# A decoder layer on one core: cross probabilities of two batches in one tile, 64-row output products, and steps that stand elsewhere

## The chip, the cores and the metric

The kernel runs on one core of a Trainium2 chip. The metric is the device time of one execution in microseconds (us), the median of several runs. Before the change it is 665.8 us, the median of three runs (664.77, 665.8 and 667.24). The profile shown below is one more execution, which took 664.33 us. Its span, from the first instruction to the last, is 662.6 us.

## The reference, cut to what matters

x has 16 batches of 256 rows with 128 features, the context 16 batches of 64 rows. The layer is a causal self-attention with 16 heads, a cross-attention with one head, and a feed-forward network of eight experts whose outputs are weighed by an entmax gate. Each part is added to x.

```python
x = x + attn(_layernorm(x))            # 16 heads of 8, causal, its own layernorm before Wo
# cross-attention: k = v = ctx, q = layernorm(x)
scores = einsum('bqd,bkd->bqk', qp, kp) * scale
probs  = softmax(scores, axis=-1)      # over the 64 context rows of the query's own batch
ctx    = einsum('bqk,bkd->bqd', probs, vp)
x = x + einsum('bqd,ed->bqe', ctx, Wo) + bo
...
gates = entmax_bisect(logits)          # exact threshold over 8 experts here
h = relu(einsum('td,edf->etf', xt, W1) + b1)
y = einsum('etf,efd->etd', h, W2) + b2
x = x + einsum('etd,te->td', y, gates)
```

## The kernel before

The batches are worked on in eight pairs (512 rows, as four tiles of 128). A pair passes through three parts: Z (layernorm, projections, row maxima of the scores), A (the rest of the self-attention, the cross-attention) and X (gates and experts). The parts are a software pipeline: a round does X of one pair, A of the next and Z of the one after that. A first phase without X fills the pipeline. Then come rounds 1 to 6 with all three parts (2 to 6 are a hardware loop), round 7 with X and A, and round 8 with X alone. YT adds a pair's expert output.

Each engine has its own program in order, made from the tables `Z_STEPS`, `A_STEPS` and `X_STEPS`. A row has a step, its number, its PSUM bank and, for each engine that takes part, a number: the whole part is a slot (0 to 33), and the fraction orders the steps within it. In slot t TensorE runs the first product of chunk t (called F(t) below: three 512-column matmuls into `h_ps`), the steps with a fraction under .5, the second product of chunk t-2 (S(t-2), three matmuls into `y_ps`), and then the steps with .5 or more. ScalarE rounds the hidden rows (H(t)), VectorE makes their remainder (L(t), `h_lo`). F(t) and S(t-2) wait for L(t-2). Nothing is reordered at run time: a step that waits holds up everything behind it on its engine.

The steps that the change touches:

- SC n: scores of two heads each (an even and an odd n together fill banks s and t); ScalarE takes exponentials into `prob`, GpSimd masks them (L902, each mask adds one to `prob_made`).
- TH 0 to 2: GpSimd's threshold for the gates (L934 to L964), after LG's logits on TensorE and VectorE.
- PV n: value products. Each has two halves; the second half of PV1 waits until the masks of SC6 and SC7 are made.
- MAX n: score maxima. An even and an odd n are one block of TensorE in banks s and t, four groups of 32 rows side by side; VectorE reduces each (L1657). A block waits until both banks were read by their last readers. MT: the maxima are transposed and split (L1664, L1666).
- XS, PT, XO: cross scores, the transposes of the exponentials `cp` and the product with `vo` (values times output matrix). `cp` has one 128x128 block for each of the four tiles, and a batch's 64 context rows fill only its half of it (`h0`): the other half is zero. PT transposes four blocks, ScalarE and VectorE split all 512 columns, and XO makes three products for each tile. VectorE adds XO's result to x1 (L1698).
- SA, NA, T3: statistics, normalisation and transposes; T3's split `fT_hi`, `fT_lo` feeds F(0) of the next round. SZ: statistics of the pair in Z.

PSUM has eight banks: s and t of two banks each, m, two of `h_ps`, one `y_ps`. A step takes a bank when all earlier users of it are drained.

```python
h0 = (k // 2) * C
last = act.activation(cp[:, k, h0:h0 + C], ps_of[buf][:, k * C:(k + 1) * C], ACT.Exp, ...)
```

Of the kernel before, what the change touches and what calls it, by code (L numbers as in the profile page):

```python
# [65 lines left out]
class Step(NamedTuple):  # L66
# [64 lines left out]
    Step("SA", 1, "-", dve=20.01, pool=4.75),
    Step("NA", 1, "-", act=23.01),
    Step("T2", 0, "m", pe=24.51, act=24.01, dve=24.01),
    Step("XS", 0, "m", pe=26.01, act=26.01, dve=25.01),
    Step("PT", 0, "s", pe=27.02, act=27.01, dve=26.04),
    Step("SA", 2, "-", dve=28.04, pool=6.25),
    Step("XO", 0, "m", pe=28.52, dve=28.03),
    Step("NA", 2, "-", act=31.01),
    Step("T3", 0, "m", pe=32.52, act=31.02, dve=31.02),
    Step("RL", 0, "-", sp=1),  # L140
]
# [3 lines left out]
    Step("LG", 0, "s", pe=1.01, dve=1.01),  # L145
    Step("TH", 1, "-", pool=1.25),
# [266 lines left out]
def bass_decoder_layer(nc, x, ctx_in, wq, wk, wv, wo, gamma, beta, xwk, xwv, xbv, xwq, xbq, xwo, xbo,  # L413
# [6 lines left out]
    with ctx:  # L420
# [15 lines left out]
        zeros = sb("zeros", [NJ, 1, P])  # L436
# [1376 lines left out]
```

## Time and profile before

| | us |
|---|---|
| median of three runs | 665.8 |
| profiled execution | 664.33 |
| its span | 662.6 |
| ahead of round 1's first F(0) | 100.16 |
| round 6 (467.24 to 540.80) | 73.56 |
| round 7 (540.80 to 607.43) | 66.63 |
| round 8 and the end (607.43 to 662.60) | 55.17 |

TensorE is busy 618.6 us, 93% of the span, VectorE 70%, ScalarE 62%, GpSimd 55%. The granted TensorE clock is 0.991 in the mean. Rounds 2 to 6 repeat within 0.15 us, so one of them, round 6, is read for all. A matmul's shown duration overlaps the next one's: what a matmul costs is read from start to start.

### The profile page before, as it was taken

How to read it: one execution, taken by the hardware profiler on the slowest of the kernel's cores; microseconds unless marked ns; L12 is line 12 of the kernel's file. 1: busy time of each engine (PE TensorE's matmuls, PEld its weight loads, DVE VectorE, ACT ScalarE, POOL GpSimd, SP SyncE). 2: the span in 40 equal slices, each digit the busy share in tenths (PEclk: the TensorE clock that was granted, in tenths of full speed). 3: DMA queues.
4: the chain of work that ended last, by engine and by line, in shares of the span. 5: the costliest groups of instructions: out<-in, count | busy, mean ns of one | idle time of the engine just before them, and what ended most of it. 6: DMA issues, size and time to landing. Idle time of an engine off the chain costs nothing.

```text
span 662.6 us, 15729 instructions
## 1 busy us (share of the span) xinstructions
PE 618.6 (93%) x5263; PEld 459.8 (69%) x5263; DVE 464.3 (70%) x996; ACT 408.0 (62%) x780; POOL 363.9 (55%) x599
## 2 busy tenths in 40 slices
PE   5488879999999999999999999999999999998997
PEld 3355557777677767777678767777677767776775
DVE  4495984679747986689747986599557984656544
ACT  4239476755777566755766557755776567665543
POOL 8625565445663737444763746544753756464363
PEclk9889999999999999999999999999999999999999
DMA  6705100530027000630036000720045000700230
GB/s 187 230 17 169 45 4 18 127 117 4 19 45 208 10 8 14 151 107 2 18 67 191 0 20 0 162 95 2 18 98 159 2 2 6 159 2 1 55 88 16
DMA packets 39195, 43.76 MB, mean 66 GB/s; under 512 B 2922, under 2 KB 23670, under 8 KB 39158
## 3 DMA queue, kind: packets, MB, share of 16 engines
q1 hardware_dynamic: 39158, 43.28, 24.5%
q8 instruction: 22, 0.36, 0.2%
q14 instruction: 15, 0.12, 0.1%
HBM read 10.04 MB, written 2.10 MB: 18 GB/s over the span
## 4 chain that ended last, share of the span: by engine, by line
PE 77%; DVE 8%; ACT 6%; POOL 3%; issue 2%; DMA 2%; SPq 2%; ACTq 0%; DVEq 0%; POOLq 0%
PE h_ps L1038 10%; PE y_ps L1038 9%; PE h_ps L1040 8%; PE h_ps L1039 8%; PE y_ps L1040 8%; PE y_ps L1039 8%; DVE negmax L1657 5%; PE sbuf_m L1149 5%; PE sbuf_s L1132 3%; PE sbuf_s L1104 2%; ACT prob L1462 2%; PE sbuf_s L1149 2%; PE sbuf_s L1053 1%; PE sbuf_s L1066 1%; PE sbuf_m L1038 1%
## 5 line engine op out<-in xcount | busy, mean ns | idle before, releaser
L1773 DVE SCALAR_TENSOR_TENSOR h_lo<-h_ps,h_hi 128x512 fp32r<-128x512 f32 x256 | 172.2, 682 | 120.3 <-ACT h_hi L1481 119.4
L1481 ACT ACTIVATE h_hi<-h_ps 128x512 fp32r<-128x512 f32 x256 | 152.1, 601 | 129.7 <-PE h_ps L1040 127.7
L1038 PE MATMUL h_ps<-fT_lo,w_hi 128*128 128x512 f32 x256 | 111.6, 436 | 4.1 <-DVE fT_lo L1626 2.7
L902 POOL TENSOR_SCALAR_AFFINE_SELECT prob<-prob 128x512 f32<-128x512 f32 x128 | 79.8, 642 | 60.7 <-ACT prob L1462 57.2
L1462 ACT ACTIVATE prob<-sbuf_s 128x768 f32<-128x768 f32 x124 | 95.2, 813 | 25.7 <-PE sbuf_s L1132 25.7
L1038 PE MATMUL y_ps<-h_lo,w_hi 128*128 128x512 f32 x255 | 106.9, 419 | 1.5 <-ACT y_sb L1490 1.5
L1657 DVE TENSOR_REDUCE negmax<-sbuf_s 128x4 f32<-128x1024 f32 (+1 forms) x91 | 106.9, 1212 | 0.1
L1039 PE MATMUL h_ps<-fT_hi,w_lo 128*128 128x512 f32 x256 | 101.2, 395 | 0.0
L1040 PE MATMUL h_ps<-fT_hi,w_hi 128*128 128x512 f32 x256 | 101.1, 395 | 0.0
L1040 PE MATMUL y_ps<-h_hi,w_hi 128*128 128x512 f32 x255 | 100.8, 395 | 0.0
L1039 PE MATMUL y_ps<-h_hi,w_lo 128*128 128x512 f32 x255 | 100.7, 395 | 0.0
L909 POOL TENSOR_TENSOR vareps_a<-mv_a,eps_t 128x4 f32<-128x4 f32 (+1 forms) x27 | 5.4, 200 | 157.5 <-DVE mv_a L1592 157.5
L983 POOL TENSOR_TENSOR y_sb<-y_sb,gate_b 128x512 f32<-128x512 f32 x55 | 70.9, 1290 | 11.9 <-ACT y_sb L1490 11.9
L986 POOL TENSOR_TENSOR acc<-acc,y_sb 128x512 f32<-128x512 f32 x55 | 70.7, 1286 | 4.3
L1038 PEld LDWEIGHTS h_ps<-fT_lo,w_hi 128*128 128x128 f32 x256 | 48.0, 188 | 19.9 <-DVE fT_lo L1626 4.0
L1038 PEld LDWEIGHTS y_ps<-h_lo,w_hi 128*128 128x128 f32 x255 | 47.9, 188 | 17.8 <-DVE h_lo L1773 3.5
L1040 PEld LDWEIGHTS h_ps<-fT_hi,w_hi 128*128 128x128 f32 x256 | 48.1, 188 | 11.5
L1040 PEld LDWEIGHTS y_ps<-h_hi,w_hi 128*128 128x128 f32 x255 | 47.9, 188 | 11.5
L1039 PEld LDWEIGHTS y_ps<-h_hi,w_lo 128*128 128x128 f32 x255 | 48.1, 188 | 7.6
L1490 ACT ACTIVATE y_sb<-y_ps,biasT 128x512 f32<-128x512 f32 x63 | 43.6, 691 | 15.5 <-PE y_ps L1040 13.1
L1039 PEld LDWEIGHTS h_ps<-fT_hi,w_lo 128*128 128x128 f32 x256 | 48.3, 189 | 6.3
L1149 PE MATMUL sbuf_m<-prob,v_t 128*32 128x128 f32 (+1 forms) x704 | 33.2, 329 | 0.0
(449 smaller groups left out, 1046.2 us busy)
## 6 DMA issues: line engine op xcount, KB each, us to landing
gate_b<-gT SPq DMA_DIRECT2D x64, 256.0 KB, 4.9
stacks<-qk SPq DMA_DIRECT2D x42, 256.0 KB, 2.5
gate_b<-in_L_ffn_W_dram SPq DMA_DIRECT2D x8, 512.0 KB, 6.1
x_r<-in_x_dram SPq DMA_DIRECT2D x8, 256.0 KB, 4.0
x_t<-in_x_dram SPq DMA_DIRECT2D x7, 256.0 KB, 2.7
out_dram<-sums SPq DMA_DIRECT2D x7, 256.0 KB, 4.4
w_hi<-qk SPq DMA_DIRECT2D x3, 256.0 KB, 4.5
w_lo<-qk SPq DMA_DIRECT2D x3, 256.0 KB, 5.4
```

The source lines that it names most:

```text
L902: pool.affine_select(out=v, in_=v, compare_op=ALU.is_ge, fill=0.0, base=0, pattern=[[0, 2], [0, 2], [1, P]], channel_multiplier=-1).then_i ...
L983: mark(pool.tensor_tensor(y, y, gate_b[:, e, :], ALU.mult))
L986: pool.tensor_tensor(acc[:, :], acc[:, :], y, ALU.add).then_inc(summed, 1)
L1038: pe.matmul(out_ap, w_hi, m_lo, start=start, stop=False)
L1039: pe.matmul(out_ap, w_lo, m_hi, start=False, stop=False)
L1040: return pe.matmul(out_ap, w_hi, m_hi, start=False, stop=stop)
L1149: last = pe.matmul(o[:, 0:S] if first else o[:, P:S], tile[:, c:c + VW], blocks(prob[:, (2 * n + v) % PG, j, :], first), start=first and v ...
L1462: act.activation(pair_of_heads(n), halves[buf][:, :, 0:3 * P], ACT.Exp).then_inc(free[buf], 1)
L1481: act.activation(h_hi[:, c % HB, :], h_ps[:, c % 2, :], ACT.Relu).then_inc(hhi_made, 1)
L1490: act.activation(y_sb[:, e % YB, :], y_ps[:, :], ACT.Identity, bias=biasT[:, e:e + 1]).then_inc(y_made, 1)
L1657: dve.tensor_reduce(negmax[:, tile, :].rearrange("p (j g) -> p j g", g=NG)[:, j:j + 2, gs], halves[buf].rearrange("p j (g s) -> p j g s", ...
L1773: dve.scalar_tensor_tensor(out=h_lo[:, c % HB, :], in0=h_ps[:, c % 2, :], scalar=0.0, in1=h_hi[:, c % HB, :], op0=ALU.max, op1=ALU.subtrac ...
```

## The change

- `cp`: in the rounds the tiles k and k+2, one of each batch, share a block (`k % 2`), since their context rows fill different halves. PT then makes two transposes in place of four, and its split has 256 columns in place of 512.
- XO: each of the two batches has its 64 rows of the array. Twelve products of 64 rows and 128 columns replace twelve of 128 rows; the two batches go to the two banks of s, where one bank (m) held all before.
- VL, a new step on SyncE's queue behind RL and ahead of K, copies the pair's rows of `vo_hi` and `vo_lo` to a fixed tile `vo_now` (two transfers from SBUF to SBUF); XO waits for it.
- The memset of `zeros` goes; the transfer that clears rows of the stacks reads a row of the stacks. `odd` and `tilt` lie in another tile.
- Many steps get other numbers. T1, PT and TA move to bank m, Q to t, XO to s, BT 2 and 3 change places.

```diff
-    Step("PT", 0, "s", pe=27.02, act=27.01, dve=26.04),
+    Step("PT", 0, "m", pe=27.02, act=26.0118, dve=27.0385),
...
-    Step("XO", 0, "m", pe=28.52, dve=28.03),
+    Step("XO", 0, "s", pe=28.52, dve=28.5248),
...
+    Step("VL", 0, "-", sp=1.1),
...
-            if s.name not in SPLIT_HALVES:
+            if s.name == "PT" and not ph.first:
+                return slice(0, S)
...
+                if name == "VL":
+                    for k in "ab" if ph.f is not None and ph.g is None else "a":
+                        sp.wait_ge(var_made[k], ph.a * 3 * NT)
+                    for k, src in enumerate((vo_hi, vo_lo)):
+                        sp.dma_start(words(vo_now[:, k:k + 1, :]), words(src[:, bass.ds(ph.a, 1), :])).then_inc(vo_loaded, 16)
...
-                    last = transposes(dst, cp, ph.tiles(n))
+                    last = transposes(dst, cp, ph.tiles(n) if ph.first else range(NT // 2))
...
+                        pe.wait_ge(vo_loaded, ph.a * 32)
+                        for q in range(2):
+                            w = slice(q * P, (q + 1) * P)
+                            for p, (c, o) in enumerate(((cpT_hi, vo_now_lo), (cpT_lo, vo_now_hi), (cpT_hi, vo_now_hi))):
+                                for b in range(2):
+                                    r = slice(b * C, (b + 1) * C)
+                                    last = pe.matmul(halves[buf][:, b, w], c[r, w], o[r, :], start=(p == 0), stop=(p == 2))
...
-                        last = act.activation(cp[:, k, h0:h0 + C], ps_of[buf][:, k * C:(k + 1) * C], ACT.Exp,
+                        last = act.activation(cp[:, k if ph.first else k % 2, h0:h0 + C], ps_of[buf][:, k * C:(k + 1) * C], ACT.Exp,
...
+                    if not ph.first:
+                        dve.wait_ge(batch_done, ph.a)
+                        o = src[:, k * E:(k + 1) * E] if ph.first else halves[buf][:, k // 2, k % 2 * E:(k % 2 + 1) * E]
```

What the numbers do is seen in the order on the engines. GpSimd at the start of a round, before (L922 ends TH0, the four L902 are the masks of SC4 to SC7, L943 to L956 are TH1, L959 begins TH2):

```order
L922 TENSOR_TENSOR power<-halves 128x12
L902 AFFINE_SELECT prob<-prob 128x2x256 x4
L943 TENSOR_SCALAR disc<-power 128x4
L944 TENSOR_TENSOR disc<-power 128x4
L945 TENSOR_TENSOR part<-below,power 128x32
L948 TENSOR_TENSOR disc<-disc,power 128x4
L950 TENSOR_TENSOR disc<-disc 128x4
L952 TENSOR_SCALAR disc<-disc 128x4
L954 TENSOR_TENSOR root<-disc,half 128x4
L956 TENSOR_TENSOR bound<-power,root 128x4
L959 TENSOR_TENSOR part<-part,bound 128x32
```

The same stretch of GpSimd after the change (nine lines were added above it, L911 is the mask):

```order
L931 TENSOR_TENSOR power<-halves 128x12
L911 AFFINE_SELECT prob<-prob 128x2x256 x2
L952 TENSOR_SCALAR disc<-power 128x4
L953 TENSOR_TENSOR disc<-power 128x4
L954 TENSOR_TENSOR part<-below,power 128x32
L957 TENSOR_TENSOR disc<-disc,power 128x4
L959 TENSOR_TENSOR disc<-disc 128x4
L961 TENSOR_SCALAR disc<-disc 128x4
L963 TENSOR_TENSOR root<-disc,half 128x4
L965 TENSOR_TENSOR bound<-power,root 128x4
L911 AFFINE_SELECT prob<-prob 128x2x256 x2
L968 TENSOR_TENSOR part<-part,bound 128x32
```

The masks of SC6 and SC7 moved behind the eight operations of TH1. TensorE ahead of PV1, before: F(5), SC8 (L1132), S(3), PV1 (L1149):

```order
L1038 MATMUL h_ps<-fT_lo,w_hi 128x512
L1039 MATMUL h_ps<-fT_hi,w_lo 128x512
L1040 MATMUL h_ps<-fT_hi,w_hi 128x512
L1132 MATMUL sbuf_s<-stacks 128x2x128 x4
L1132 MATMUL sbuf_s<-stacks 128x128 x4
L1038 MATMUL y_ps<-h_lo,w_hi 128x512
L1039 MATMUL y_ps<-h_hi,w_lo 128x512
L1040 MATMUL y_ps<-h_hi,w_hi 128x512
L1149 MATMUL sbuf_m<-prob,v_t 32x256 x4
L1149 MATMUL sbuf_m<-prob,v_t 32x128 x4
```

And after: S(3), SC8 (L1141), F(6), PV1 (L1158):

```order
L1047 MATMUL y_ps<-h_lo,w_hi 128x512
L1048 MATMUL y_ps<-h_hi,w_lo 128x512
L1049 MATMUL y_ps<-h_hi,w_hi 128x512
L1141 MATMUL sbuf_s<-stacks 128x2x128 x4
L1141 MATMUL sbuf_s<-stacks 128x128 x4
L1047 MATMUL h_ps<-fT_lo,w_hi 128x512
L1048 MATMUL h_ps<-fT_hi,w_lo 128x512
L1049 MATMUL h_ps<-fT_hi,w_hi 128x512
L1158 MATMUL sbuf_m<-prob,v_t 32x256 x4
L1158 MATMUL sbuf_m<-prob,v_t 32x128 x4
```

PV1 moved behind one more first product, F(6). Late in the round, TensorE behind F(27), before: MT0 (L1205), PT0 (L1053), S(25); the block of MAX8 and MAX9 follows two products later, behind S(26), with XO0 behind it:

```order
L1205 MATMUL sbuf_m<-ident,negmax 16x128 [waits free_t,free_s,free_m]
L1205 MATMUL sbuf_m<-ident,negmax 16x128
L1053 MATMUL sbuf_s<-ident,cp 128x128 [waits free_m,free_s]
L1053 MATMUL sbuf_s<-ident,cp 128x128 x3
L1038 MATMUL y_ps<-h_lo,w_hi 128x512 [waits hlo_made]
```

And after: MT0 (L1214), the block of MAX8 and MAX9 (L1113, L1121), PT0 (L1062), S(25); XO0 stays behind S(26):

```order
L1214 MATMUL sbuf_m<-ident,negmax 16x128 [waits free_t,free_s,free_m]
L1214 MATMUL sbuf_m<-ident,negmax 16x128
L1113 MATMUL sbuf_s<-stacks 128x256 [waits free_t,free_s]
L1113 MATMUL sbuf_s<-stacks 128x256 x7
L1121 MATMUL sbuf_s<-causal,ident_bf 32x2x32 x16
L1062 MATMUL sbuf_m<-ident,cp 128x128 [waits free_m]
L1062 MATMUL sbuf_m<-ident,cp 128x128
L1047 MATMUL y_ps<-h_lo,w_hi 128x512 [waits hlo_made]
```

The block moved ahead of PT0, next to the block of MAX6 and MAX7 that fills the same banks. At the round's end TensorE had F(31), S(29), S(30), MT1, T30, S(31), SC2; now it has F(31), S(29), T30, S(30), MT1, S(31), SC2, and ScalarE's NA2 stands ahead of H(31). VectorE reduces MAX8 ahead of L(27), MAX9 behind L(28); SZ0 moves from slot 8 to slot 2, SA1 ahead of L(20). On ScalarE PT0's split stands ahead of H(27).

## Rows read from the trace of the kernel before

**Rows 1.** Windows, round 6: length, busy us of PE, PEld, DVE, ACT, POOL, clock, DMA.
```profile
467.24:540.80 73.56, 72.39 (x639) 54.39 (x639) 55.70 (x119) 47.97 (x94) 41.06 (x68) 1.00 0.24 62
```
**Rows 2.** Waits of TensorE in round 6: total us, times, longest.
```profile
PE h_ps L1038 <- DVE fT_lo L1626: 0.7, 2, 0.3
PE sbuf_s L1205 <- DVE negmax L1657: 0.5, 1, 0.5
PE sbuf_s L1104 <- ACT prob L1462: 0.3, 1, 0.3
```
**Rows 3.** Windows of VectorE alone, from its first maxima to round 6's end.
```profile
513.57:540.74 27.17, 26.41 (x46) 1.00 0.00 1
```
**Rows 4.** Timeline of GpSimd, round 6: TH0, four masks, TH1's first and last.
```profile
473.77 0.30 POOL L934 TENSOR_SCALAR moments<-excess 128x32 f32<-128x32 f32 x1 [1.62 <-DVE excess L1725]
...
475.95 2.41 POOL L902 TENSOR_SCALAR_AFFINE_SELECT prob<-prob 128x512 f32<-128x512 f32 x4 [0.26 <-ACT prob L1462]
478.33 0.23 POOL L943 TENSOR_SCALAR disc<-power 128x4 f32<-128x4 f32 x1
...
480.99 0.20 POOL L956 TENSOR_TENSOR bound<-power,root 128x4 f32<-128x4 f32 x1
```
**Rows 5.** Timeline of TensorE, round 6: F(5), SC8, S(3), PV1.
```profile
476.31 0.40 PE L1038 MATMUL h_ps<-fT_lo,w_hi 128*128 128x512 f32 x1
476.54 0.40 PE L1039 MATMUL h_ps<-fT_hi,w_lo 128*128 128x512 f32 x1
...
477.10 0.45 PE L1132 MATMUL sbuf_s<-stacks 32*128 32x256 f32 x8
477.48 0.50 PE L1038 MATMUL y_ps<-h_lo,w_hi 128*128 128x512 f32 x1
477.81 0.40 PE L1039 MATMUL y_ps<-h_hi,w_lo 128*128 128x512 f32 x1
...
478.37 1.51 PE L1149 MATMUL sbuf_m<-prob,v_t 128*32 128x256 f32 x32
```
**Rows 6.** Timelines of round 1: GpSimd's TH1 begins, TensorE's PV1 begins.
```profile
110.08 0.23 POOL L943 TENSOR_SCALAR disc<-power 128x4 f32<-128x4 f32 x1
...
111.26 1.07 PE L1149 MATMUL sbuf_m<-prob,v_t 128*32 128x256 f32 x20
```
**Rows 7.** Timeline of TensorE, round 6: PT0, S(25), MAX8's block, XO's first, F(29), SC0.
```profile
526.27 0.62 PE L1053 MATMUL sbuf_s<-ident,cp 128*128 128x128 f32 x4
526.65 0.48 PE L1038 MATMUL y_ps<-h_lo,w_hi 128*128 128x512 f32 x1
...
528.92 0.51 PE L1104 MATMUL sbuf_s<-stacks 32*128 32x256 f32 x8
...
529.68 0.30 PE L1038 MATMUL sbuf_m<-vo_lo,tT_hi 128*128 x1
...
531.07 0.45 PE L1038 MATMUL h_ps<-fT_lo,w_hi 128*128 128x512 f32 x1
...
532.60 0.45 PE L1132 MATMUL sbuf_s<-stacks 32*128 32x256 f32 x8
```
**Rows 8.** Timeline of VectorE, round 6: MAX6 and 7, PT0, XO, MAX10 and 11.
```profile
524.97 2.34 DVE L1657 TENSOR_REDUCE negmax<-sbuf_s 128x8 f32<-128x1024 f32 x2
...
528.01 0.67 DVE L1632 TENSOR_TENSOR tT_lo<-sbuf_s,tT_hi 128x512 fp32r<-128x512 f32 x1
...
532.13 1.10 DVE L1698 SCALAR_TENSOR_TENSOR sums<-sbuf_m,crec,x 128x128 f32<-128x128 f32 x4
...
536.00 2.34 DVE L1657 TENSOR_REDUCE negmax<-sbuf_s 128x4 f32<-128x1024 f32 x2
```
**Rows 9.** Timeline of TensorE, end of round 7: T30, which waits for ScalarE.
```profile
605.39 0.63 PE L1053 MATMUL sbuf_m<-ident,ln 128*128 128x128 f32 x4 [0.91 <-ACT ln L1404]
```
**Rows 10.** Timeline of SyncE, round 6: RL's transfer. Page, part 6: the stacks' transfers.
```profile
500.37 0.81 SPq L799 DMA_DIRECT2D x_r<-in_x_dram  x1
...
stacks<-qk SPq DMA_DIRECT2D x42, 256.0 KB, 2.5
```

More of the change, by code:

```diff
@@ new lines @@
+    Step("SC", 7, "t", pe=3.0139, act=3.5185, pool=1.25),
+    Step("SC", 8, "s", pe=5.5098, act=5.026, pool=1.75),
+    Step("SC", 9, "t", pe=5.5208, act=5.0331, pool=2),
+    Step("PV", 1, "m", pe=6.0082, act=5.5127),
+    Step("SC", 10, "s", pe=6.0214, act=7.5176, pool=2.25),
+    Step("SC", 11, "t", pe=6.5211, act=9.5104, pool=2.5),
+    Step("SC", 12, "s", pe=10.5096, act=9.5327, pool=2.75),
+    Step("SC", 13, "t", pe=10.5166, act=9.5381, pool=3.25),
+    Step("PV", 2, "m", pe=10.5214, act=9.5512),
@@ L607, in bass_decoder_layer @@
         gate_turn = sem("gate_turn")
+        batch_done = sem("batch_done")
+        vo_loaded = sem("vo_loaded")
         stored = sem("stored")
@@ L721, in stack_rows @@
                 if ph.first:
-                    sp.wait_ge(const_made if n else const0_made, 5 if n else 2)
+                    sp.wait_ge(const_made if n else const0_made, 4 if n else 2)
                 drained(sp, ph, "Q", n)
@@ L740, in spread_cells @@
             def spread_cells(pair):
-                sp.wait_ge(const_made if pair else const0_made, 5 if pair else 2)
+                sp.wait_ge(const_made if pair else const0_made, 4 if pair else 2)
                 sp.wait_ge(cells_made, 5)
@@ L877, in masks @@
                 pool.memset(cp[:, :, :], 0.0).then_inc(const_made, 1)
-                pool.memset(zeros[:, :, :], 0.0).then_inc(const_made, 1)
             def cells():
@@ L1240, in step @@
                         drained(pe, ph, "vo")
-                    for k in ph.tiles(n):
-                        w = slice(k * P, (k + 1) * P)
-                        v = bass.ds(ph.a, 1)
-                        last = three(dst[:, w], cpT_hi[:, w], cpT_lo[:, w], vo_hi[:, v, :], vo_lo[:, v, :])
+                    v = bass.ds(ph.a, 1)
+                    if ph.first:
+                        for k in ph.tiles(n):
+                            w = slice(k * P, (k + 1) * P)
+                            last = three(dst[:, w], cpT_hi[:, w], cpT_lo[:, w], vo_hi[:, v, :], vo_lo[:, v, :])
+                    else:
+                        pe.wait_ge(vo_loaded, ph.a * 32)
[5 more added lines that the diff above has]
+                                    last = pe.matmul(halves[buf][:, b, w], c[r, w], o[r, :], start=(p == 0), stop=(p == 2))
+                                    if q == 1 and p == 2 and b == 0:
+                                        last.then_inc(batch_done, 1)
                 if name == "LG":
```

99 lines of the change are left out of this document (45 added, 54 removed).

## The prediction

> **What bounds the kernel now.** I read the windows of the rounds first, to see which engine is never free. In round 6 TensorE is busy 72.39 of 73.56 us at full clock [rows 1]; rounds 2 to 6 are copies of it. The waits come next: TensorE waits three times a round, 0.28 us for ScalarE's exponentials ahead of MAX10, 0.50 us for the last maxima ahead of MT1, and a little over 0.3 us for `fT_lo` at the next F(0); the second wait in the `fT_lo` row is that of the round's own first F(0) [rows 2]. That is 1.1 us, all at the end. Then the same round by VectorE alone: from 513.57 to the round's end it works 26.41 of 27.17 us [rows 3]. So a round has two parts. Up to the first maxima TensorE sets the pace and the others have slack; from there on VectorE's row of reductions and remainders ends last, and TensorE keeps only about 1 us of slack to it. A stall of TensorE in the first part lengthens the round in full. In the second part a delay counts if it leaves VectorE without work.
>
> **The change part by part.** There are seven rounds with the new cross-attention, 1 to 7. I make the sum against the profiled execution's 664.33 us.
>
> *Masks behind TH1 (first part).* Before, GpSimd ends TH0, makes four masks from 475.95 to 478.36, and then runs TH1 from 478.33 to 481.19, 2.86 us [rows 4]. It can't begin earlier: it stood idle 1.62 us until VectorE's `excess` came, and the change leaves that chain as it is. Now two masks end at 475.95 + 1.20 = 477.15, TH1 follows until 480.0, a mask block begins 0.26 us after such small operations (the idle time in the mask row), and two masks take 1.2: the mask of SC7 is made at 481.5, where it was 478.4. TensorE's PV1 began at 478.37 and took 1.51, so its second half began at about 479.1 (half of 1.51; an estimate). F(6) now stands ahead of it, three products of 0.23 from start to start [rows 5]: 479.8. The second half waits 481.5 - 479.8 = 1.7 us. Behind it on TensorE stand SC10, S(4), F(7) and everything else; nothing passes it. ScalarE has H(6) behind PV1's copy, VectorE L(6), but both have slack there. In round 1 the pair of times is 111.26 + 0.70 + 0.75 = 112.7 against 110.1 + 3.1 = 113.2 [rows 6]: 0.5 us. Sum over the rounds: 6 x 1.7 + 0.5 = **+10.7**. Bounds: if PV1's first half is only a third of it the wait is 1.95 (+1.5 in all); if small operations on GpSimd go a fifth faster it is 1.1 (-3.6).
>
> *MAX8 early, XO in bank s (second part, rounds 1 to 6).* The block of MAX8 and 9 now stands where PT0 began, 526.27 [rows 7], and needs banks s and t, which VectorE reads until 524.97 + 2.34 = 527.31 [rows 8]. TensorE waits 1.0 us there. VectorE is not idle meanwhile: MT0 lies ahead of MAX8 on it, until PT0's 528.01. The block takes 0.76 (528.92 to 529.68), so it ends about 0.1 us after VectorE could use it. PT0's remainder has half the columns, up to 0.3 less of its 0.67; L(27) and L(28) may cost 0.1 each, since H(27) now stands behind PT0's split on ScalarE. VectorE thus comes to XO between 532.1 and 532.4, where it was 532.13. But XO now lies in s. Before, SC0 started at 532.60 as soon as TensorE reached it, since MAX8 and 9 were drained and XO lay in m. Now SC0 waits until VectorE has read XO, 1.10 us from 532.3: 533.5 with the signal, +0.9 for SC0. Its two exponentials run behind it, MAX10 waits for them (it waits 0.28 already [rows 2]), and VectorE's MAX10 slips from 536.00 to about 536.7. From there to F(0) VectorE's work is one row of 4.7 us, so the round ends +0.7 later. T30 ahead of S(30) and MT1 can't help: MT1 is set by the end of MAX11 and `fT_lo` stands behind MT1 on VectorE. Sum: 6 x 0.7 = **+4.2**. Bounds: -0.3 a round, if SC0's wait is absorbed and the shorter remainder counts, and +1.0, if all of TensorE's wait at MAX8 counts: -1.8 to +6.0.
>
> *XO and PT on TensorE.* Two of PT's four transposes fall away: half of 526.27 to 526.65, 0.19 us. XO's twelve products took 1.39 (529.68 to 531.07 [rows 7]). No row shows two groups of 64 rows. The nearest is MAX8's block: eight products in four groups of 32 rows pass in 0.44 with 256 columns (within its 0.51), SC8's eight of 256 and 128 in 0.38 (477.10 to 477.48 [rows 5]), so 0.048 each. Two groups in place of four give 0.7 to 0.95 for twelve; no overlap at all gives the old 1.39. I take 0.8, a saving of 0.6. The array's change of tile size must come off: S(3) behind SC8 has 0.33 between its first two starts where F(5) has 0.23, and F(5) to SC8 takes 0.79 where three products take 0.69, so 0.10 on either side [rows 5]. XO now has such a pair of its own, 0.2, for net 0.6 - 0.2 + 0.19 = 0.6 a round. In rounds 1 to 6 this is worth nothing, because TensorE waits at SC0 for longer than that; were the cover gone it would be -3.6 in all.
> [...]
>
> *Round 7* has no maxima, and its end is a chain: XO, statistics, NA2, T30, F(0). T30 waits 0.91 us for `ln` [rows 9]. XO ends about 0.6 earlier, and NA2 no longer stands behind H(31), some 0.3. T30 then waits ahead of S(30) in place of behind it, which alone neither gains nor costs, since F(0) hangs on T30. **-0.9**, bounds 0 and -1.2.
>
> *At nothing.* VL's two transfers stand behind RL, which is issued at 500.37 for 0.81 us [rows 10]; XO reads them at 529.68, and a 256 KB transfer of the stacks lands in 2.5 us, so 25 us cover them. Were K's stacks held up by two more issues of 0.8 each, the maxima at 513 would still be later. The memset is in the first phase, on GpSimd, beside other work. SZ0 in slot 2 puts 1.2 us ahead of L(3); by the idle time of VectorE there this fits, and if it doesn't F(5) loses up to 0.3. The moves of Q, K and SA1 keep TensorE's work the same.
>
> Sum: 664.33 + 10.7 + 4.2 - 0.9 = 678.3 us. The profiled execution was 1.5 us below the median of the runs shown, so I put the median at **679**.
>
> **The rivals.**
> 1. *Only the masks cost.* SC0's wait and MAX8's are absorbed by slack that PV1's stall gives ScalarE and VectorE: 664.3 + 10.7 - 0.9, and up to 1.8 less: 672 to 674. For it speaks that VectorE's own work in the second part shrinks; against it that both waits hang on VectorE itself, which begins its row with TensorE's first maxima and so gains nothing from a late TensorE.
> 2. *The masks come in time.* GpSimd makes SC7's mask by 479.8, 1.7 us sooner than the rows give. This needs `excess` sooner by that much, and no edit touches it. Then 664.3 + 4.2 - 0.9 = 667.6, slower by 0.5% at most.
> 3. *Faster: TensorE alone sets the round.* What it no longer has to do counts in full, 0.6 in each of six rounds, with 0.9 in round 7: 664.3 - 3.6 - 0.9 = 659.8, and 653 if the 1.1 us of waits at the round's end go too. It decides at one place, PV1's second half: the saving of 0.6 a round outweighs the masks' lateness only if that is under 0.6, so if TH1 takes 1.1 us less of GpSimd than its 2.86. For it speaks 93% of TensorE; against it is that six such waits are read directly from two rows.
> 4. *The 64-row products don't overlap.* XO stays at 1.39 and adds its mode changes, +0.2. TensorE's slack at SC0 hides it in rounds 1 to 6, and round 7 gains only 0.1 to 0.3: 679. It changes the sum by under 1 us.
>
> **How the numbers follow.** The forecast with both waits, rival 4 in it, has a chance of 0.65: 675 to 684, by the bounds of its terms taken together in quadrature. Rival 1 has 0.17, rival 2 0.05, rival 3 0.08; 0.05 is left for something that I don't see. For 8 in 10 the range takes in the forecast and rival 1 with a shorter TH1: **669 to 685**. A difference under 0.5% (3.3 us) can't be told from none here. Faster by more than that: rival 3 and a part of the rest, 0.09. Within: rival 2, 0.06. Slower: 0.85.
>
> **What would show it.** Right: TensorE idles about 1.7 us before the second half of L1158 in each round, ended by GpSimd's mask (L911), and GpSimd's last of L952 to L965 ends ahead of the third mask. TensorE waits about 1 us at MAX8's block for `negmax`, and at SC0 (L1141 behind S(27)) for VectorE's sums. Rounds 2 to 6 take 75.5 to 76.3 us. Wrong: rounds at 73 us or below, no idle time at L1158, or SC0 that starts right behind S(27). The prediction fails above all if masks of SC6 and SC7 reach PV1 before 480, which the order on GpSimd doesn't allow unless TH0 starts earlier.

## The result, and the profile after the change

The changed kernel takes 682.06 us (median of four runs, 680.57 to 683.30) against 665.79 for the kernel before beside it: 1.0242 times as long, 95% interval 1.0214 to 1.027. Forecast were 679 and 669 to 685. The profiled execution took 683.3 us with a span of 681.6, 19.0 more than that of before.

The windows of rounds 1, 2, 6 and 7 come first, and then two short stretches (length, busy time of PE, PEld, DVE, ACT and POOL, granted clock, DMA):

```profile
100.77:177.58 76.81, 74.35 (x632) 55.27 (x632) 54.17 (x118) 46.98 (x91) 37.19 (x64) 0.96 0.22 59
177.58:255.07 77.49, 73.67 (x636) 54.80 (x637) 55.57 (x119) 47.83 (x93) 41.18 (x68) 0.98 0.23 63
482.77:558.53 75.76, 72.02 (x637) 53.55 (x637) 55.45 (x119) 47.71 (x92) 41.16 (x68) 1.00 0.23 62
558.53:626.45 67.92, 63.63 (x438) 47.24 (x438) 36.64 (x88) 42.80 (x83) 38.30 (x62) 1.00 0.19 43
101.40:108.20 6.80, 6.80 (x54) 4.95 (x53) 3.42 (x9) 1.36 (x3) 0.82 (x4) 0.50 0.08 23
193.50:196.90 3.40, 3.40 (x9) 2.65 (x8) 1.47 (x4) 1.38 (x3) 1.23 (x2) 0.50 0.00 0
```

Round 6 takes 75.76 against 73.56 [rows 1], 2.20 more, and TensorE's busy time in it fell by 0.37, from 72.39 to 72.02. So it waits longer. Rounds 1 and 2 lose more, 4.0 each against 72.85 and 73.45 before, and the granted clock, the column before the last two, says why: their clock is 0.96 and 0.98, since 6.80 us of round 1 and 3.40 us of round 2 ran at 0.50. Before, no stretch of rounds 1 to 7 did. Taken at half speed, that is work of 3.4 us done in 6.8, and of 1.7 in 3.4, an estimate of about 5 of the 19.0 us (512-column products that start 0.23 apart at full clock start 0.43 apart in the stretch of round 2). The medians differ by 16.3 only. The profiled execution of before had a mean clock of 0.991, more than any of the 75 runs of that kernel beside the experiments below (0.974 to 0.989), so the two profiles set a clean execution against a more usual one.

TensorE's waits in round 6, which answer to [rows 2]:

```profile
PE sbuf_m L1158 <- POOL prob L911: 1.5, 1, 1.5
PE sbuf_s L1113 <- DVE negmax L1678: 0.9, 1, 0.9
PE sbuf_s L1141 <- DVE sums L1722: 0.6, 1, 0.6
PE sbuf_m L1062 <- ACT ln L1425: 0.3, 1, 0.3
PE h_ps L1047 <- DVE fT_lo L1647: 0.3, 1, 0.3
```

The first is the wait for the masks, 1.5 in each of rounds 2 to 7 (9.1 us together). The second is MAX8's block, the third SC0. The waits of before for the exponentials ahead of MAX10 (0.28) and for the last maxima ahead of MT1 (0.50) are gone from the list. GpSimd's timeline in the same round, which answers to [rows 4]:

```profile
489.18 0.30 POOL L943 TENSOR_SCALAR moments<-excess 128x32 f32<-128x32 f32 x1 [1.62 <-DVE excess L1749]
...
491.36 1.23 POOL L911 TENSOR_SCALAR_AFFINE_SELECT prob<-prob 128x512 f32<-128x512 f32 x2 [0.26 <-POOL power L931]
492.56 0.22 POOL L952 TENSOR_SCALAR disc<-power 128x4 f32<-128x4 f32 x1
...
495.20 0.20 POOL L965 TENSOR_TENSOR bound<-power,root 128x4 f32<-128x4 f32 x1
495.65 1.24 POOL L911 TENSOR_SCALAR_AFFINE_SELECT prob<-prob 128x512 f32<-128x512 f32 x2 [0.25 <-POOL bound L965]
```

TH0 begins 1.62 us after GpSimd fell idle, as before; two masks, TH1, then the pair that PV1 waits for, which is done at 496.89. TensorE's timeline at PV1, F(6)'s first product and then the two halves; behind it the second half of before, whose first began at 478.37 [rows 5]:

```profile
493.65 0.50 PE L1047 MATMUL h_ps<-fT_lo,w_hi 128*128 128x512 f32 x1
...
494.55 0.86 PE L1158 MATMUL sbuf_m<-prob,v_t 128*32 128x256 f32 x16
496.94 0.86 PE L1158 MATMUL sbuf_m<-prob,v_t 128*32 128x256 f32 x16 [1.53 <-POOL prob L911]
```

```profile
479.04 0.83 PE L1149 MATMUL sbuf_m<-prob,v_t 128*32 128x256 f32 x16
```

From start to start the halves stood 0.67 apart and now stand 2.39 apart: the second comes 1.72 late. The idle time of 1.53 is shorter because the first half's shown 0.86 reaches past the point where the next product could start.

The same timeline behind MT0, which answers to [rows 7]: MAX8's block, PT0, the last product of S(26), the first of XO's, F(29) and SC0:

```profile
544.41 0.51 PE L1113 MATMUL sbuf_s<-stacks 32*128 32x256 f32 x8 [0.93 <-DVE negmax L1678]
...
545.18 0.44 PE L1062 MATMUL sbuf_m<-ident,cp 128*128 128x128 f32 x2
...
547.31 0.40 PE L1049 MATMUL y_ps<-h_hi,w_hi 128*128 128x512 f32 x1
547.64 0.33 PE L1263 MATMUL sbuf_s<-vo_now,tT_hi 64*128 64x128 f32 x2
...
547.91 0.39 PE L1263 MATMUL sbuf_s<-vo_now,tT_hi 64*128 64x128 f32 x4
548.14 0.28 PE L1263 MATMUL sbuf_s<-vo_now,tT_lo 64*128 64x128 f32 x2
...
548.45 0.50 PE L1047 MATMUL h_ps<-fT_lo,w_hi 128*128 128x512 f32 x1
548.79 0.39 PE L1048 MATMUL h_ps<-fT_hi,w_lo 128*128 128x512 f32 x1
...
550.76 0.45 PE L1141 MATMUL sbuf_s<-stacks 32*128 32x256 f32 x8 [0.65 <-DVE sums L1722]
```

PT0 has two transposes and takes 0.19 to the next start. XO lasts from 547.64 to 548.45, 0.81, where twelve products of 128 rows took 1.39 [rows 7]. Four of the 64-row products pass in 0.23 (547.91 to 548.14), where one of the old ones took about 0.12: by these starts the groups of 64 rows do run side by side. From the last product of S(26) to XO it is 0.33 from start to start, and F(29)'s first two starts stand 0.34 apart, 0.10 and 0.11 over the 0.23 between the products of F and S. Other gaps are longer too. The second products of S(25) and F(29) in before's timeline, to be read with the first ones in [rows 7]:

```profile
526.97 0.39 PE L1039 MATMUL y_ps<-h_hi,w_lo 128*128 128x512 f32 x1
...
531.36 0.39 PE L1039 MATMUL h_ps<-fT_hi,w_lo 128*128 128x512 f32 x1
```

S(25) stands behind PT0's transposes and F(29) behind XO's twelve products, all of them of 128 rows, and the first two starts are 0.32 and 0.29 apart all the same. So the 0.10 and 0.11 stand beside a change of tile size, but how much of them comes of it isn't shown.

VectorE's timeline, XO, L(30) and MAX10:

```profile
549.42 1.12 DVE L1722 SCALAR_TENSOR_TENSOR sums<-sbuf_s,crec,x 128x128 f32<-128x128 f32 x4
...
553.28 0.69 DVE L1797 SCALAR_TENSOR_TENSOR h_lo<-h_ps,h_hi 128x512 fp32r<-128x512 f32 x1 [0.84 <-ACT h_hi L1502]
553.88 1.22 DVE L1678 TENSOR_REDUCE negmax<-sbuf_s 128x4 f32<-128x1024 f32 x1
```

XO is read from 549.42 on; SC0 waits for the end of that. Before L(30) VectorE is idle for 0.84 us until ScalarE has the hidden rows of F(30), which stands behind SC0.

### The profile page after: what moved, and what is told of

Read it like the earlier page. It is cut to its first block, busy times and chain, and to the rows that moved or that the text cites. A ratio compares the mean times of both kernels' runs of the same rounds, so it can differ in the third digit from the quotient of the medians.

```text
span 681.6 us, 15722 instructions
## 1 busy us (share of the span) xinstructions
PE 620.8 (91%) x5249; PEld 457.0 (67%) x5249; DVE 463.6 (68%) x996; ACT 406.8 (60%) x780; POOL 364.7 (54%) x598
## 4 chain that ended last, share of the span: by engine, by line
PE 31%; issue 30%; POOL 17%; DVE 10%; ACT 7%; DMA 2%; SPq 2%; POOLq 1%; ACTq 0%; DVEq 0%
PE y_ps L1047 4%; PE h_ps L1047 4%; DVE negmax L1678 3%; PE y_ps L1049 3%; PE y_ps L1048 3%; PE sbuf_m L1158 3%; POOL rstd_a L921 3%; PE h_ps L1049 3%; PE h_ps L1048 3%; POOL prob L911 3%; POOL y_sb L992 2%; ACT prob L1483 2%; ACT ln L1425 2%; PE sbuf_s L1141 2%; POOL acc L995 2%
## 5 line engine op out<-in xcount | busy, mean ns | idle before, releaser
L911 POOL TENSOR_SCALAR_AFFINE_SELECT prob<-prob 128x512 f32<-128x512 f32 x128 | 80.4, 640 | 77.7 <-ACT prob L1483 71.1
L1047 PE MATMUL y_ps<-h_lo,w_hi 128*128 128x512 f32 x255 | 108.4, 425 | 1.4 <-ACT y_sb L1511 1.4
L1158 PE MATMUL sbuf_m<-prob,v_t 128*32 128x128 f32 (+1 forms) x704 | 35.7, 339 | 9.1 <-POOL prob L911 9.1
```

The lines of the kernel that those rows point to most:

```text
L911: pool.affine_select(out=v, in_=v, compare_op=ALU.is_ge, fill=0.0, base=0, pattern=[[0, 2], [0, 2], [1, P]], channel_multiplier=-1).then_i ...
L1047: pe.matmul(out_ap, w_hi, m_lo, start=start, stop=False)
L1158: last = pe.matmul(o[:, 0:S] if first else o[:, P:S], tile[:, c:c + VW], blocks(prob[:, (2 * n + v) % PG, j, :], first), start=first and v ...
```

## The experiments

Each set ran on another chip, beside runs of the kernel before on that chip (medians 667.5 to 668.1); ratios are to those, with 95% intervals. Since half-clock stretches at the start (10.2 us in e1's profile, none in before's between 45 us and round 1) make whole times uneven, I also compare round 6 of each profile, at a granted clock of 1.00 in all of them. It is one execution of each kernel; where the clock is full, rounds 3 to 6 of a profile agree within 0.2. Padded is explained at e6.

| kernel | MAX8 | XO | masks | round 6, us | median, us | ratio |
|---|---|---|---|---|---|---|
| before | old place | 128 rows, m | old | 73.56 | 667.5 to 668.1 | 1 |
| after | early | 64 rows, s | late | 75.76 | 682.06 | 1.0242 |
| e1 | early | 64 rows, s | old | 74.12 | 671.22 | 1.0052 (1.0032 to 1.0071) |
| e2 | old place | 128 rows, m | late | 75.90 | 685.66 | 1.028 (1.0257 to 1.0304) |
| e3 | early | old code, m | old | 75.02 | 678.07 | 1.0149 (1.0127 to 1.0171) |
| e4 | early | old code, s | old | 74.80 | 678.26 | 1.0151 (1.0128 to 1.0175) |
| e5 | early | 64 rows, s | old | 74.35 | 671.63 | 1.0056 (1.0035 to 1.0077) |
| e6 | old place | padded, m | old | 72.92 | 662.27 | 0.9907 (0.9884 to 0.993) |
| e7 | early | padded, m | old | 74.02 | 671.04 | 1.0039 (1.0023 to 1.0054) |
| e8 | early | old code, m | old | 75.29 | 680.15 | 1.0166 (1.0137 to 1.0194) |
| e9 | early | padded, m | old | 73.99 | 670.17 | 1.0039 (1.0019 to 1.006) |
| e10 | old place | padded, m | old | 72.93 | 664.30 | 0.9951 (0.9932 to 0.9971) |
| e11 | early | 64 rows, s | late, PV1 later | 75.58 | 679.82 | 1.0206 (1.0175 to 1.0237) |
| e12 | old place | padded, 12 products | old | 73.35 | 666.99 | 0.998 (0.9963 to 0.9997) |

After's ratio is from its own set. All other steps stand as in the changed kernel in e1, e3, e4, e7 and e11, as before in e2, e5, e6, e8, e9 and e12. e10 mixes them.

**The masks: e1, e2.** One undoes them alone, one makes them alone.

```diff
 e1, in the changed kernel, the numbers alone (e2: the opposite, in the kernel before)
-    SC 6: pool=1      SC 7: pool=1.25   TH 1: pool=0.75
+    SC 6: pool=0.75   SC 7: pool=1      TH 1: pool=1.25
```

e1: 

> The changed kernel with TH1 and the masks of SC6 and SC7 in their old order on GpSimd, nothing else. Theory (the masks' lateness costs what TensorE waits at PV1): the wait of 1.5 us at PV1's second half is gone in rounds 1 to 7; six of 1.53 and 0.5 are 9.7 us, so 672.4; and if the half-clock stretch of round 2 (193.5 to 196.9) came of that wait, 1.6 less, 670.8, with round 1's too 668. Rounds 2 to 6 are 74.2 to 74.4. Rival (the stall gave the others time that they now lack): 674 to 680, and other waits of TensorE grow.

e2: 

> The kernel before with TH1 ahead of the masks of SC6 and SC7 on GpSimd, nothing else. Theory: PV1's second half, reached at about 479.1 in round 6, waits for a mask made at 481.2 to 481.5, 2.1 to 2.4 us in rounds 2 to 7 and about 1.2 in round 1: +14 to +16, 680 to 682, without any half-clock stretch beyond those of before. If stalls of this length lower the clock as in round 2 of the changed kernel, 2 to 10 more. Rival (later slack takes up the stall): under 674.

In e1 the wait at PV1 is gone, no other takes its place, and round 6 is 1.64 shorter than after's, nearly the 1.72 by which PV1's second half came late. In e2 PV1, which stands one first product earlier there, waits 2.35 between its halves; the timeline of TensorE in its round 6:

```profile
494.07 0.86 PE L1149 MATMUL sbuf_m<-prob,v_t 128*32 128x256 f32 x16
497.27 0.86 PE L1149 MATMUL sbuf_m<-prob,v_t 128*32 128x256 f32 x16 [2.35 <-POOL prob L902]
```

Round 6 of e2 is 2.34 longer than that of before: a stall here counts in full, or nearly. Both as the theory had it, but for round 1, where e2 doesn't wait at PV1 (1.2 were expected; 6.8 us at half clock stand ahead of it). e2's median of 685.66 lies above 680 to 682. Its +14 to +16 were counted from about 666, and the runs of before beside it took 668.1; and in the profiled execution the clock fell behind two of the six stalls and at the start of round 1. The windows of its round 3, of the stretch behind that round's stall and of round 6:

```profile
252.07:329.55 77.48, 73.95 (x639) 55.55 (x639) 54.95 (x119) 48.09 (x94) 41.18 (x68) 0.98 0.22 59
268.00:271.70 3.70, 3.70 (x11) 2.88 (x10) 0.69 (x1) 1.81 (x4) 1.99 (x4) 0.54 0.00 0
...
482.95:558.85 75.90, 72.36 (x639) 54.32 (x639) 54.94 (x119) 47.99 (x94) 41.15 (x68) 1.00 0.23 60
```

**What e1 still loses: e3, e4.** Round 6 of e1 is 0.56 slower than that of before, and rounds 1 to 6 of its profile are 4.1 slower together. I took the wait of SC0 on bank s for the cause, and put the old code into m or s to test it.

```diff
 e3, in e1 (e4: the same with XO in "s")
-    Step("XO", 0, "s", pe=28.52, dve=28.5248),
+    Step("XO", 0, "m", pe=28.52, dve=28.5248),
-    Step("VL", 0, "-", sp=1.1),
...
-                    last = transposes(dst, cp, ph.tiles(n) if ph.first else range(NT // 2))
+                    last = transposes(dst, cp, ph.tiles(n))
...
+                    for k in ph.tiles(n):
+                        w = slice(k * P, (k + 1) * P)
+                        last = three(dst[:, w], cpT_hi[:, w], cpT_lo[:, w], vo_hi[:, v, :], vo_lo[:, v, :])
```

e3: 

> e1 with the old cross-attention code: four blocks of the exponentials, four transposes, twelve products of 128 rows in bank m, no transfer of value rows; all steps stand as in the changed kernel. Theory (what is left of the loss in rounds 1 to 6 is SC0's wait for VectorE to read XO in bank s): SC0 starts right behind S(27), rounds 2 to 6 are 73.4 to 73.7, 0.7 a round less than e1, and round 7 loses 0.8: e1 less 3 to 4. Rival (MAX8's early wait of 0.9 us costs, not the bank): as e1 or up to 1 us slower, rounds of 74.2 and over.

e4: 

> e3 with XO in bank s in place of m. Theory: SC0 waits 0.6 to 0.7 for VectorE's read again, rounds 2 to 6 are 74.2 to 74.4, so e3 plus 4; against e1 the products take 0.6 longer, which VectorE's later arrival at XO hides in rounds 1 to 6, and round 7 loses 0.8: e1 plus 0.5 to 1.5. Rival (the bank doesn't matter, the 64-row form does): within 1 us of e3.

The theory fell. SC0 does start right behind S(27) in e3, but the round is 0.9 longer than e1's, not 0.7 shorter, and e4 is no slower than e3, as e4's rival had it; SC0 doesn't wait there either: XO itself waits 0.5 for PT's remainder, VectorE reads it at once, and F(29) and S(27) cover the reading. e3's rival had the rounds right, but not the time: e3 takes 6.9 more than e1, not up to 1. TensorE's waits in round 6 of e3:

```profile
PE sbuf_s L1110 <- DVE negmax L1663: 0.9, 1, 0.9
PE sbuf_m L1044 <- DVE tT_lo L1638: 0.6, 1, 0.6
...
```

MAX8's block waits 0.9 here as well, and XO now waits 0.6 for PT's remainder, which came late behind it. Either the wait at MAX8 counts after all, or other moved steps do.

**MAX8 with its neighbours, and the cross part alone: e8, e5.** MAX8 and 9 don't move by themselves in these runs: PT goes to bank m, its split on ScalarE moves from behind H(27) to ahead of it, and its remainder on VectorE from ahead of L(27) to behind it (XO and SA2 only get numbers that keep them behind MAX9).

```diff
 e8, in the kernel before (e5: with XO in "s", VL and the new cross code)
-    Step("MAX", 8, "s", pe=28.51, dve=28.01),
-    Step("MAX", 9, "t", pe=28.52, dve=28.02),
+    Step("MAX", 8, "s", pe=27.0118, dve=26.513),
+    Step("MAX", 9, "t", pe=27.0201, dve=28.5169),
...
-    Step("PT", 0, "s", pe=27.02, act=27.01, dve=26.04),
-    Step("SA", 2, "-", dve=28.04, pool=6.25),
-    Step("XO", 0, "m", pe=28.52, dve=28.03),
+    Step("PT", 0, "m", pe=27.02, act=26.0118, dve=27.0385),
+    Step("SA", 2, "-", dve=28.5464, pool=6.25),
+    Step("XO", 0, "m", pe=28.52, dve=28.5248),
```

e8: 

> The kernel before, old code, with MAX8 and 9 early and PT, XO and SA2 at the numbers of the changed kernel, PT and XO in m. Theory, formed on e3: TensorE waits 0.9 at MAX8 and 0.5 to 0.6 at XO for PT's remainder, and both count: rounds 2 to 6 are 74.6 to 75.1, before plus 6 to 9. The prediction on record (the wait at MAX8 is mostly hidden): at most 0.2 a round, before plus 0 to 1.5.

e5: 

> The kernel before with the new cross-attention alone: its code, VL, MAX8 and 9 early, PT in m, XO in s, SA2, with the numbers that these have in the changed kernel; every other step and every mask where it was. Theory (what the changed kernel loses behind the first maxima comes of these steps): MAX8 waits 0.9 and SC0 0.6 to 0.7, rounds 2 to 6 are 74.0 to 74.4, round 7 is 65.7 to 66.3, before plus 2.5 to 4. Rival (the other moved steps, T30 ahead of MT1, NA2, Q, K and SZ0, have a part in it): more than 1 us from that on either side, and rounds that differ from the 74.2 of e1.

With the old code MAX8's move and what goes with it cost 1.73 a round, more than either view had. e5 takes 74.35, near e1's 74.12: the loss is in the cross part's steps, and the other moved steps gain 0.23 in round 6 and 0.04 to 0.19 in rounds 3 to 5. The timeline of VectorE in e8's round 6, its remainders L(27) and L(30):

```profile
543.85 0.69 DVE L1773 SCALAR_TENSOR_TENSOR h_lo<-h_ps,h_hi 128x512 fp32r<-128x512 f32 x1 [0.57 <-ACT h_hi L1481]
...
551.06 0.69 DVE L1773 SCALAR_TENSOR_TENSOR h_lo<-h_ps,h_hi 128x512 fp32r<-128x512 f32 x1 [1.10 <-ACT h_hi L1481]
```

TensorE's wait of 0.94 at MAX8 comes back on VectorE as 0.57 ahead of L(27) and 1.10 ahead of L(30) (before: 0.26 at this place), both ended by ScalarE. The two differ in kind. L(30) needs F(30), which comes late on TensorE. L(27) needs H(27), and F(27) stands ahead of MAX8 and was done in time. But H(27) now stands behind PT0's split, which waits for TensorE; before, ScalarE took it 0.43 after the start of F(27)'s last product. The timelines of ScalarE, PT0's split and H(27) in e8, and H(27) before:

```profile
542.73 0.60 ACT L1452 ACTIVATE tT_hi<-sbuf_m 128x512 fp32r<-128x512 f32 x1 [3.05 <-PE sbuf_m L1053]
543.23 0.59 ACT L1481 ACTIVATE h_hi<-h_ps 128x512 fp32r<-128x512 f32 x1
```

```profile
526.26 0.60 ACT L1481 ACTIVATE h_hi<-h_ps 128x512 fp32r<-128x512 f32 x1 [0.47 <-PE h_ps L1040]
```

PT0's remainder stands behind L(27) on VectorE, so XO's wait of 0.6 on TensorE hangs on that order too. No run moves MAX8 and leaves PT's split behind H(27); how much of the 1.73 is the wait at MAX8 itself stays open.

**The saving alone: e6, e12.** To keep XO in m and every step where it was, the value rows of each batch get a tile with zero rows for the other batch; one product of 128 rows and 256 columns makes a tile of both batches.

```diff
 e6, on the steps of before
+                            o = dst.rearrange("p (b q e) -> p q b e", b=2, q=2)[:, q, :, :]
+                            last = three(o, cpT_hi[:, w], cpT_lo[:, w], vo_now_hi[:, :, :], vo_now_lo[:, :, :])
 e12, in e6
-                        for q in range(2):
+                        for k in range(NT):
+                            b, q = divmod(k, 2)
...
+                            last = three(dst[:, k * P:(k + 1) * P], cpT_hi[:, w], cpT_lo[:, w],
+                                         vo_now_hi[:, b, :], vo_now_lo[:, b, :])
```

e6: 

> The steps of before, all in their old places and banks. Two batches share a block of the exponentials and PT makes two transposes, but the value rows of each batch lie in a tile of their own with zero rows for the other batch, so that XO is six products of 128 rows and 256 columns (both batches side by side) in bank m, with no change of tile size. The rows come by four transfers behind RL, and two small memsets of GpSimd clear the tiles once, in round 1. Prediction's claim (TensorE's saving behind the first maxima is covered by its waits for VectorE): rounds 2 to 6 are 73.2 to 73.6, MT1's wait grows by what XO and PT save, round 7 gains 0.9: before less 0.5 to 3. Rival (TensorE's work there counts in full): XO 0.7 and PT 0.2 less, rounds of 72.7, before less 6.

e12: 

> e6 with XO as twelve products of 128 rows and 128 columns in place of six of 256 columns: TensorE's time at XO is that of before (1.39 in place of 0.80), PT's two transposes and half split stay. It tells which of e6's savings made its rounds 0.64 shorter than those of before. Theory (both engines set the second part by turns): SC0's wait of 0.23 takes up part of the 0.59, F(30) comes 0.36 later, ScalarE's hidden rows 30 reach VectorE too late again, and rounds 2 to 6 are 73.3 to 73.45, e6 plus 2 to 3. Rival 1 (VectorE alone, by its shorter remainder at PT): 72.9 to 73.1, as e6. Rival 2 (TensorE alone): 73.5 to 73.6, as before the change.

e6 beats both kernels, 0.9% under before. The window of its round 6, and then TensorE's timeline there: XO's first product, F(29)'s first two, SC0:

```profile
469.28:542.20 72.92, 71.68 (x630) 53.54 (x631) 55.33 (x119) 47.64 (x93) 41.07 (x68) 1.00 0.24 65
```

```profile
531.48 0.38 PE L1058 MATMUL sbuf_m<-vo_now,tT_hi 128*128 128x256 f32 x1
...
532.29 0.40 PE L1058 MATMUL h_ps<-fT_lo,w_hi 128*128 128x512 f32 x1
532.52 0.39 PE L1059 MATMUL h_ps<-fT_hi,w_lo 128*128 128x512 f32 x1
...
534.08 0.45 PE L1152 MATMUL sbuf_s<-stacks 32*128 32x256 f32 x8 [0.23 <-DVE negmax L1685]
```

The six products pass in 0.81, as fast as the twelve of 64 rows, and F(29), here of the same tile size as XO, has 0.23 between its first starts. Round 6 is 0.64 shorter than that of before, close to the rival's 72.7 and outside the 73.2 to 73.6 that the prediction allowed. TensorE saved 0.23 at PT (0.38 to 0.15) and 0.59 at XO. e12 gives XO's part back. The window of its round 6:

```profile
467.90:541.25 73.35, 72.19 (x636) 54.16 (x637) 55.42 (x119) 47.63 (x93) 41.06 (x68) 1.00 0.24 64
```

73.35 lies in the theory's 73.3 to 73.45 and in neither rival's range. So of e6's 0.64, 0.43 came of XO on TensorE alone, though TensorE still waits 0.5 at MT1 in both, and 0.21 of the rest: PT's two transposes and its half splits on ScalarE and VectorE.

**The bank: e7, e9.** The padded XO in m while MAX8 stays early, on e1's steps and on e5's.

```diff
 e7, in e1 (e9: the same in e5)
-    Step("XO", 0, "s", pe=28.52, dve=28.5248),
+    Step("XO", 0, "m", pe=28.52, dve=28.5248),
 and e6's cross code
```

e7: 

> e1 with this padded XO in bank m in place of the 64-row products in s; the steps stand as in the changed kernel. Theory (SC0's wait on bank s costs what is left): SC0 starts right behind S(27), rounds 2 to 6 are 73.5 to 73.7, e1 less 3 to 4. Rival (VectorE's row ends last anyway, and TensorE waits at MAX10, MT1 or F(0) instead): within 1 us of e1.

e9: 

> e5 with the padded XO in bank m in place of the 64-row products in s: MAX8 still early, MT1 still ahead of T30 as before the change. Theory, formed on e7 (there the wait on bank s went, but T30, which stands ahead of MT1, waited 0.7 for ScalarE in its place): with the old order at the end the gain of 0.5 at MAX10 on VectorE is kept, rounds 2 to 6 are 73.7 to 73.9, e5 less 3. Rival (the wait on bank s costs nothing, TensorE's and VectorE's row is set by MAX8's wait alone): rounds of 74.1 and over, e5 less 1.5 at most.

In e7 SC0 no longer waits for VectorE to read XO, and the round is within 0.1 of e1's; here the rival held. TensorE's waits in its round 6:

```profile
PE sbuf_s L1124 <- DVE negmax L1685: 0.9, 1, 0.9
PE sbuf_m L1073 <- ACT ln L1432: 0.7, 1, 0.7
...
```

T30, which the changed kernel puts ahead of MT1, now waits 0.7 for ScalarE and holds MT1 up. With the old order at the end, on e5's steps, part of the gain stays. The window of e9's round 6:

```profile
472.24:546.23 73.99, 71.77 (x630) 53.58 (x630) 55.66 (x119) 47.61 (x94) 40.98 (x68) 1.00 0.24 64
```

That is 0.36 under e5, between the two expectations. It is 1.07 over e6, which differs only by MAX8's place and the steps that go with it, those of e8. Half of that is there when VectorE reaches XO (65.10 after the round's start, against 64.60 in e6); the rest comes ahead of L(30), where VectorE waits 0.46 for H(30). At L(27) it waits only 0.14 here.

**Two that were to gain: e10, e11.** e10 joins the first part of e1 to the second part of e6. e11 keeps the late masks and lets PV1 stand later:

```diff
 e11, in the changed kernel, the numbers alone
-    PV 1: pe=6.0082, act=5.5127   SC 10: pe=6.0214   SC 11: pe=6.5211
+    PV 1: pe=7.0082, act=6.5127   SC 10: pe=7.0214   SC 11: pe=7.5211
```

e10: 

> The changed kernel's steps of the first part with the masks in their old order, and from MAX6 on all steps and banks as before, with the padded XO in m. Theory (e6 is the right way for the second part; the first part reaches the first maxima 0.1 a round earlier in e1 than in before): rounds 2 to 6 are 72.7 to 72.9, before less 6 to 7.5, e6 less 0 to 1.5. Rival (the first part's moves are worth nothing): as e6, before less 5.7.

e11: 

> The changed kernel with GpSimd's new order kept, but PV1 (and SC10 and 11) two products later on TensorE, behind S(4) and F(7), its copy on ScalarE behind H(6). Theory (the masks cost only what TensorE reaches PV1 too early): two products of 0.7 cover 1.4 of the 1.5, rounds 2 to 6 are 74.2 to 74.5 as in e1, about 671, and no half-clock stretch in rounds 2 to 7. Rival (ScalarE, which has PV1's copy ahead of H(7) and SC10, hands the delay on): rounds over 75, 675 and more.

e10's round 6 is that of e6 within 0.01: the first part's moves bring nothing, and round 7 takes 66.35 against 65.86. Its median is 3.4 under before, where the theory had 6 to 7.5 and the rival 5.7; round 7 is 0.5 of what is missing, and the rest stays open. e11's stall at PV1 went, and another came. The timeline of TensorE in round 6, S(4) and then PV1:

```profile
492.71 0.50 PE L1047 MATMUL y_ps<-h_lo,w_hi 128*128 128x512 f32 x1 [1.29 <-ACT y_sb L1511]
...
494.32 1.51 PE L1158 MATMUL sbuf_m<-prob,v_t 128*32 128x256 f32 x32
```

S(4) needs the bank `y_ps`, which ScalarE evicts only behind the exponentials of SC8 and SC9, as its timeline shows:

```profile
490.57 1.51 ACT L1483 ACTIVATE prob<-sbuf_s 128x768 f32<-128x768 f32 x2 [0.21 <-PE sbuf_s L1141]
491.97 0.69 ACT L1511 ACTIVATE y_sb<-y_ps,biasT 128x512 f32<-128x512 f32 x1
```

My two products of cover were not there: S(4) can't start before about 492.7 in that order, and round 6 gains 0.18 of 1.5. The time is the rival's (675 and more), by another wait than the rival named.

## Why the prediction was right, and where it was not

Round 6 as a ledger, each step one pair of kernels: before 73.56; PT's two transposes and half splits -0.21 (e12); XO at 0.81 in place of 1.39 -0.43 (e6); MAX8 early with the steps that go with it +1.07 (e9); XO in s by 64-row products +0.36 (e5); all other moved steps -0.23 (e1); masks late +1.64 (after). Sum +2.20, and 75.76 is what after takes. The prices hold along this path: on the old code MAX8's move costs 1.73 (e8), and the late masks cost 2.34 where F(6) doesn't stand ahead of PV1 (e2).

*Masks.* Right in mechanism, place and size: PV1's second half comes 1.72 late where 1.7 was forecast, and the round grows by 1.64. GpSimd's side was right: from TH0 to the late pair it is 6.47 (489.18 to 495.65), against 6.49 by my terms. PV1's first half takes 0.67 from start to start; I had taken half of 1.51. Round 1's 0.5 can't be judged: 6.80 us at half clock, just ahead of it, put TensorE behind, and PV1 didn't wait.

*Second part.* Forecast +0.7 in each of rounds 1 to 6, 4.2 together; measured +0.56 in round 6 and 4.1 together (e1). VectorE's MAX10 starts 69.48 after the round's start in e1 against 68.76 before [rows 8], later by the 0.7 of the prediction. That the size came out is luck: the terms below it were wrong and happened to cancel. MAX8's wait was to cost VectorE about 0.1: MAX8's move and what goes with it cost 1.07. "Worth nothing" for what PT and XO save: it is worth 0.64. SC0's wait as the sole cost of 0.7: it came at 0.65, and the 64-row products in s, with their two changes of tile size, cost 0.36 in all (e5 over e9). For the bank alone, the one pair that differs in nothing else (e3 at 75.02, e4 at 74.80) shows no price, but XO is late in both.

The step that failed is the reading of [rows 3]: 26.41 busy of 27.17 was taken to mean that VectorE's row ends last, with 1 us of slack for TensorE. The row hangs on TensorE at some places, through ScalarE: H(30) comes from F(30), and H(27) stands behind PT0's split where the change put it. And TensorE's waits at the round's end are for results of VectorE that hang on those products. They aren't slack of a product that stands ahead of F(30). With XO faster or slower alone (e6, e12) the round follows TensorE by three quarters (0.43 of 0.59), MT1's wait of 0.5 notwithstanding.

*XO and PT on TensorE.* 0.81 for an estimate of 0.8, 0.19 as forecast, 0.10 and 0.11 on the two sides of XO as on those of SC8 in [rows 5]. The sum had these as the price of changing the tile size (rival 4's mode changes); with 0.06 and 0.09 behind steps that change nothing, that price is an estimate of mine that no run shows by itself. Rival 4 is out.

*Round 7.* From PT0 to the next F(0) it takes 11.61 in e1 against 12.50: the -0.9 of the prediction. Of the round only 0.37 is left (66.26 in e1; 65.91 in e5, without the other moved steps). These moves, put at nothing, bring two waits of 0.2 for `h_lo` in the middle of that round in e1, absent in e5 and before; which of them does it, no run shows.

*The total.* Of 19.0 us between the profiled executions, the masks make 9.8 (6 x 1.64), the second part 4.1 in six rounds, half-clock stretches in rounds 1 and 2 about 5, and the phase ahead of round 1 0.6, less 0.4 in round 7. The prediction had 14.0 and no term for the clock. That is the likely reason why 679 fell short of 682; it isn't shown, since only one of the four runs of after was traced.

*The rivals.* Masks as the only cost (672 to 674): out, e1 is slower than before. Masks in time: out, PV1 waits in rounds 2 to 7. TensorE alone, faster: its saving is real, and e6 shows it, but the masks and MAX8's move (1.64 and 1.07 a round) outweigh its 0.64 four times over.

*The second bank.* The 64-row products with their two banks in s cost 0.36 a round (e5 over e9), and 256 columns with zero rows do the same work in the same 0.81 and in one bank. No run put the 64-row products of both batches into one bank, so what that costs isn't shown.

## What to carry to other kernels

An engine that works 97% of a stretch need not bound it alone: look at what ends its few idle moments, and if that leads back to the other engine, a saving or a wait on either counts until a run says otherwise. A wait for another engine late in a stretch is slack only for work behind the last thing that this engine waited for. A step that a table moves past another (masks past a threshold, a block up to the drain of its banks) is priced by who stands behind it on every engine that it moves on (H(27) behind PT0's split); before putting something else in the gap, see what that in turn waits for (S(4) for its bank in e11).

## What the runs showed of the hardware

The clock fell behind stalls that the same kernel elsewhere took at full clock. TensorE in round 2 of after, PV1's second half behind its stall, and products of the same kind behind it:

```profile
191.79 0.86 PE L1158 MATMUL sbuf_m<-prob,v_t 128*32 128x256 f32 x16 [1.50 <-POOL prob L911]
...
193.29 0.42 PE L1048 MATMUL y_ps<-h_hi,w_lo 128*128 128x512 f32 x1
...
193.93 0.63 PE L1047 MATMUL h_ps<-fT_lo,w_hi 128*128 128x512 f32 x1
```

The products shown at 0.40 elsewhere take 0.63, and start 0.43 apart in place of 0.23; the clock is 0.50 for 3.4 us and then full again. Of six such stalls of 1.50 to 1.53 us in after one was followed by this, of six of 2.23 to 2.35 us in e2 two (0.54 over 3.70 us in round 3, 0.50 over 3.40 us in round 5, from 421.60 on), and in none of the profiles without the stall (before, e1, e3 to e10, e12) was there a half-clock stretch in rounds 2 to 7; nor in e11, with its 1.3 at S(4). These are single executions, so the shares are rough. Further stretches of 3 to 10 us at 0.50 come between 45 us and the first microseconds of round 1 in every profile but that of before, whatever the edit (after's 101.4 to 108.2, e1's 46.8 to 57.0, e9's 50.2 to 53.6); the lower mean clocks of before's other runs (0.974 to 0.989, against the profile's 0.991) suggest that before mostly has them too. Why one execution has them where another hasn't stays open. What it means for a sum: the stall costs nearly its length in every round (1.64 for 1.72 in after, 2.34 for 2.35 in e2), and in some rounds 1.6 to 1.7 more (after's round 2 takes 77.49 against 75.76 for round 6, e2's round 3 77.48 against 75.90).
